# Scores mixed into the first inverse product of a tile, the last slot's rows turned on TensorE, zero rows held back during a weight load, and one activation issued earlier

## What is computed

```
x = x + attn(layernorm(x))        # x is 1 x 2048 x 512
  q, k, v = silu(conv4(x @ Wq)), silu(conv4(x @ Wk)), silu(conv4(x @ Wv))   # 8 heads of 64
  q, k = l2norm(q) / 8, l2norm(k); beta = sigmoid(x @ Wb)
  per token: u = beta * (v - k S);  S = S + k^T u;  o = q S
  o = o * rsqrt(mean(o*o)) * norm_w;  attn = o @ Wo
x = x + ffn(layernorm(x))
  routed: softmax gate, 2 of 4 groups, top 4 of 16 experts, (silu(x Wg) * (x Wu)) @ Wd, width 352
  shared: the same form with width 704, for every token
```

## Time and profile before

| | us |
|---|---|
| median of 3 runs | 1335.73 (1335.23 to 1336.11) |
| the profiled execution, its own time | 1335.12 |
| its span, first to last instruction | 1333.4 |
| PE busy | 1280.4 (96% of the span) |
| DVE / ACT / POOL busy | 870.3 / 373.6 / 336.8 |
| PE's granted clock, mean over the span | 0.983 of full speed |

### The profile page before, as it was taken

The page is one execution under the profiler, slowest core; times in us unless marked ns, Lnnn a source line. Parts: engine busy times, 40 slices in busy tenths (PEclk is TensorE's granted clock), DMA queues, the critical chain, the costliest instruction groups (busy, mean ns, idle before and its releaser), DMA issues.

```text
span 1333.4 us, 27815 instructions
## 1 busy us (share of the span) xinstructions
PE 1280.4 (96%) x8722; PEld 797.3 (60%) x8723; DVE 870.3 (65%) x2426; ACT 373.6 (28%) x816; POOL 336.8 (25%) x396
## 2 busy tenths in 40 slices
PE   8978999998998999999999999999999999999996
PEld 7857777776776555444444555555555555555553
DVE  4896698669659325645111577777777777777774
ACT  4745555555453323120000011111111111111111
POOL 1211224322233122214653012122121222212121
PEclk9989999999997999999999999999999999999997
DMA  5525852743467494265456556666665656564420
GB/s 160 97 42 103 122 118 70 154 117 74 106 135 172 121 236 106 99 212 209 177 204 232 131 128 132 137 132 139 135 138 130 135 132 134 128 139 71 71 51 1
DMA packets 208515, 171.08 MB, mean 128 GB/s; under 512 B 71472, under 2 KB 160560, under 8 KB 208432
## 3 DMA queue, kind: packets, MB, share of 16 engines
q1 hardware_dynamic: 135056, 114.16, 33.4%
q0 software_dynamic: 16496, 34.23, 13.1%
q10 hardware_dynamic: 56880, 21.54, 7.8%
HBM read 91.06 MB, written 82.73 MB: 130 GB/s over the span
## 4 chain that ended last, share of the span: by engine, by line
PE 54%; DVE 2%; issue 0%; POOLq 0%; DVEq 0%; ACT 0%
PE pD L2202 15%; PE pG L2182 14%; PE pU L2191 14%; PE pG L2146 3%; PE pU L2146 3%; PE pD L2165 3%; DVE ups L2092 1%; PE pU L2140 1%; PE pD L2160 0%; POOLq L1917 0%; DVE w L1804 0%; DVE w L1805 0%; DVE route_keep L1803 0%; DVE qf L1816 0%; DVE q L1823 0%
## 5 line engine op out<-in xcount | busy, mean ns | idle before, releaser
L2092 DVE STREAM_TRANSPOSE ups<-a 32x96 f32<-32x96 f32 (+1 forms) x1264 | 330.4, 261 | 42.7
L1989 POOL DMA_INDIRECT out<-y,ix x79 | 123.0, 1557 | 481.3 <-ACT y L2045 322.7
L2202 PE MATMUL pD<-w,ups 128*128 (+1 forms) x474 | 219.3, 599 | 3.6 <-DVE ups L2092 3.6
L2182 PE MATMUL pG<-w,xsT 128*128 x632 | 199.9, 458 | 0.0
L2191 PE MATMUL pU<-w,xsT 128*128 x632 | 199.9, 459 | 0.0
L2182 PEld LDWEIGHTS pG<-w,xsT 128*128 128x128 f32 x632 | 119.5, 189 | 88.4 <-issue 37.6
L2191 PEld LDWEIGHTS pU<-w,xsT 128*128 128x128 f32 x632 | 120.1, 190 | 66.9
L954 PE MATMUL pProj<-front_region 128*128 128x256 f32 x624 | 154.5, 390 | 2.0 <-ACT front_region L697 1.6
L2202 PEld LDWEIGHTS pD<-w,ups 128*128 128x128 f32 (+1 forms) x474 | 90.8, 192 | 98.0 <-issue 81.7
L1331 DVE SCALAR_TENSOR_TENSOR front_region<-front_region,cw 128x256 f32<-128x256 f32 x288 | 133.4, 504 | 12.3 <-ACT front_region L733 8.9
L2045 ACT ACTIVATE y<-pD,wq 128x512 f32<-128x512 f32 x79 | 54.3, 687 | 255.2 <-PE pD L2202 245.5
(11 more groups left out here) (240 smaller groups left out, 1575.9 us busy)
## 6 DMA issues: line engine op xcount, KB each, us to landing
w<-in_up_T SPq DMA_DIRECT2D x16, 1408.0 KB, 6.8
slot_rows<-zeros SPq DMA_DIRECT2D x79, 266.0 KB
xs<-slot_rows ACTq DMA_DIRECT2D x316, 64.0 KB
w<-in_down_T SPq DMA_DIRECT2D x16, 512.0 KB, 8.8
front_region<-in_L_attn_hidden_states SPq DMA_DIRECT2D x16, 256.0 KB, 3.5
x2r<-in_L_attn_hidden_states SPq DMA_DIRECT2D x16, 256.0 KB, 4.8
partial_sums<-x2r SPq DMA_DIRECT2D x16, 256.0 KB, 3.7
x_normed<-x2n SPq DMA_DIRECT2D x16, 256.0 KB, 2.2
```

The costliest lines, as they stand in the source:

```text
L1989: pool.indirect_dma_start(out=flat, out_offset=bass.IndirectOffsetOnAxis(ap=ix[1 - par][:, 0:1], axis=0), in_=y[1 - par][:, :], in_offset= ...
L2092: dve.transpose(aT[par][B * to:B * to + B, 0:n, rows], a[rows, 0:len(IC) * P].rearrange("p (c n) -> p c n", c=len(IC))[:, 0:n, B * to:B * ...
L2182: mm = pe.matmul(pG[0][:, 0:I], xsT[par][:, k, :], w[:, bass.ds(slot, 1), 2 * I * k:2 * I * k + I], start=(k == 0), stop=(k == DC - 1))
L2202: mm = pe.matmul(pYq[:, :], aT[1 - par][0:m, c, :], down[0:m, :, UPW + D * c:UPW + D * (c + 1)], start=(c == 0), stop=(c == 2))
```

## The change

Four edits, independent of each other.

1. `scores(u+1)` no longer stands alone ahead of the projection. For u from 0 to 14 its 16 matmuls are placed between the 8 of `hop_u(u, 0)`, in a new function `hop_u_and_scores`. DVE's `mask_scores(u+1)` moves from the end of slot 1 to the start of slot 2.
2. For the last slot PE turns the rows of `a` itself with three transposes against an identity (`turn_last`), placed in the down product of the slot before; ACT and DVE copy the results; the last down product has a bank of its own (`pYlast`). POOL builds the identity after its routing constants.
3. `zero_rows` is not called in step 10 from slot 2 on, nor in step 11 in slots 0 and 1. Six pieces move to the end of the list: step 15 slot 1 and step 16 slots 0 to 4.
4. `shared_silu` stands ahead of the copies of its slot on ACT.

```diff
-                    if u >= 0 and not (u % 4 == 3 and s >= 2) and not (u % 4 == 1 and s >= 4) and not (u % 4 == 2 and s < 1):
+                    if u >= 0 and not (u % 4 == 3 and s >= 2) and not (u % 4 == 1 and s >= 4) and not (u % 4 == 2 and s < 1) \
+                            and not (u == 10 and s >= 2) and not (u == 11 and s < 2):
                         zero_rows()
...
+                    for n in range(EARLY_UNITS):
+                        if fill_slot(u, s) == event_slot(gate_end(n)):
+                            shared_silu(n)
                     if tile_ok(u) and s == 0 and u < FUSED:
                         x_copy(u)
...
+            def hop_u_and_scores(t):
+                if t < FUSED:
+                    pe.wait_ge(s_TT, t + 1)
+                else:
+                    pe.wait_ge(s_X, 2 * t + 2)
+                pe.wait_ge(s_R, 2 * t + 1)
+                scores_wait(t + 1)
+                r = cols(0, C)
+                for n in range(HH):
+                    for f, between in ((0, ((1, 1), (0, 0), (1, 0))), (1, ((0, 1),))):
+                        g = HH * f + n
+                        u_mm = pe.matmul(pC[r, f, cols(n)], TT[t % TT_RING][r, cols(g)], Rs[r, cols(g)], start=True, stop=True)
+                        if (n, f) == (HH - 1, 1):
+                            u_mm.then_inc(s_Up, 1)
+                        for sf, sc in between:
+                            s_mm = score(t + 1, n, sf, sc)
+                s_mm.then_inc(s_Pp, 1)
...
-                    if s == 1 and tile_ok(u + 1):
-                        scores(u + 1)
+                    if s == 1 and u == -1:
+                        scores(0)
...
-                    if tile_ok(u) and s in (1, 4):
+                    if s == 1 and tile_ok(u) and tile_ok(u + 1):
+                        hop_u_and_scores(u)
+                    elif tile_ok(u) and s in (1, 4):
                         hop_u(u, s // 3)
...
+                    if s == 2 and tile_ok(u) and tile_ok(u + 1):
+                        mask_scores(u + 1)
...
-                    if s == 1 and tile_ok(u + 1):
-                        mask_scores(u + 1)
+                    if s == 1 and u == -1:
+                        mask_scores(0)
...
+    pA, pYlast = [pG[1], pU[1], pD[3]], pD[1]
...
+                if isinstance(q, int) and q == NQ - 1:
+                    act.wait_ge(s_yp, NQ - 2)
+                    for c in (0, 2):
+                        act.wait_ge(s_lap, c + 1)
+                        act.activation(aT[par][0:IC[c], c, :], pA[c][0:IC[c], 0:P], ACT.Copy).then_inc(s_laT, 1)
...
-                    turn_gated(q, par)
+                    if isinstance(q, int) and q == NQ - 1:
+                        dve.wait_ge(s_yp, NQ - 2)
+                        dve.wait_ge(s_lap, 2)
+                        dve.tensor_copy(aT[par][:, 1, :], pA[1][:, 0:P]).then_inc(s_laT, 1)
+                    else:
+                        turn_gated(q, par)
...
+            def turn_last():
+
+                pe.wait_ge(s_eye, 2)
+                pe.wait_ge(s_a, NQ)
+                for c in range(3):
+                    pe.transpose(pA[c][0:IC[c], 0:P], a[:, P * c:P * c + IC[c]], eye[:, :]).then_inc(s_lap, 1)
...
                     for c in range(3):
                         m = IC[c]
-                        mm = pe.matmul(pYq[:, :], aT[1 - par][0:m, c, :], down[0:m, :, UPW + D * c:UPW + D * (c + 1)],
+                        if isinstance(q, int) and q == NQ - 1 and c == 2:
+                            turn_last()
+                        mm = pe.matmul((pYlast if end(q) else pYq)[:, :], aT[1 - par][0:m, c, :], down[0:m, :, UPW + D * c:UPW + D * (c + 1)],
                                        start=(c == 0), stop=(c == 2))
```

More of the change, by code:

```diff
@@ L905, in _ @@
                         w_copy(u + 1)
-                    for n in range(EARLY_UNITS):
-                        if fill_slot(u, s) == event_slot(gate_end(n)):
-                            shared_silu(n)
                     if (u, s) == ROUTE_AT:
@@ L1008, in gram, with scores_wait, score @@
                 mm.then_inc(s_G, 1)
+            def scores_wait(t):
+                least(pe, s_N, capped(t + 5 if t % 2 and not late_gram(t - 2) else t + 4))
+            def score(t, n, f, c):
+                p = t // 2
+                return pe.matmul(pG[cols(c, C), f, cols(n)], kq[p % KQ_RING][half(f), n, tok(t, c)],
+                                 kq[p % KQ_RING][half(f), DC + n, tok(t, c)], start=True, stop=True)
             def scores(t):
-                p = t // 2
-                least(pe, s_N, capped(t + 5 if t % 2 and not late_gram(t - 2) else t + 4))
+                scores_wait(t)
                 for n in range(HH):
@@ L1015, in scores @@
                         for f in range(2):
-                            mm = pe.matmul(pG[cols(c, C), f, cols(n)], kq[p % KQ_RING][half(f), n, tok(t, c)],
-                                           kq[p % KQ_RING][half(f), DC + n, tok(t, c)], start=True, stop=True)
+                            mm = score(t, n, f, c)
                 mm.then_inc(s_Pp, 1)
@@ L1849, in experts @@
     g, a = sb("g", [P, I]), sb("a", [P, len(IC) * P])
+    eye = sb("eye", [P, P])
     y = [sb(f"y{i}", [P, D]) for i in range(2)]
@@ L1867, in experts @@
     s_add, s_ex, s_base = sem("rows_added"), sem("meta_taken"), sem("base_stored")
+    s_eye, s_lap, s_laT = sem("identity2"), sem("last_gated_psum"), sem("last_gatedT_ready")
     s_xT, s_gp, s_g, s_up, s_a, s_aT, s_yp, s_y = (sem(n) for n in (
@@ L1965, in _ @@
             route_pool(pool)
+            pool.memset(eye[:, :], 0.0).then_inc(s_eye, 1)
+            pool.wait_ge(s_eye, 1)
+            pool.affine_select(out=eye[:, :], in_=eye[:, :], compare_op=ALU.not_equal, fill=1.0,
+                               base=0, pattern=[[-1, P]], channel_multiplier=1).then_inc(s_eye, 1)
             for n in BY_POOL:
@@ L2044, in body @@
                         act.wait_ge(s_add, (q - 2) * 16)
-                    act.activation(y[1 - par][:, :], pYq[:, :], ACT.Copy, scale=wq[1 - par][:, 0:1]).then_inc(s_y, 1)
+                    act.activation(y[1 - par][:, :], (pYlast if end(q) else pYq)[:, :], ACT.Copy, scale=wq[1 - par][:, 0:1]).then_inc(s_y, 1)
             route_act(act)
@@ L2195, in body @@
                 if not first(q):
-                    pe.wait_ge(s_aT, BLOCKS * BLOCKS * q)
-                    wait_pos(pe, s_y, q - 1)
+                    if end(q):
+                        pe.wait_ge(s_laT, 3)
+                    else:
+                        pe.wait_ge(s_aT, BLOCKS * BLOCKS * q)
+                        wait_pos(pe, s_y, q - 1)
                     if isinstance(q, int) and q == 1:
```

## The result

| | before | after |
|---|---|---|
| median, us | 1334.78 (19 runs) | 1327.67 (19 runs) |
| ratio, 95% interval | | 0.9947 (0.9939 to 0.9955) |
| profiled execution, us | 1335.12 | 1325.61 |
| granted clock in it | 0.983 | 0.988 |

A forecast was written before the change was run, and what follows sets the result against it. PE, the engine with least idle time, was taken to bound the kernel, except where DVE's inverse does. Savings of 0.5 (mix and mask), 0.9 (step 11) and 2.3 us (tail) sum to 3.7: forecast 1331.9 us, range 1328.6 to 1335.1.

The forecast's parts named there:

- The mix on PE: Attention: hop_u and scores interleaved take 1.55 us, saving 0.14 us per tile; eight steps keep it, 1.1 us.
- halves: Rival for the mixed products: matmuls of one row half don't overlap, 2.10 us per mix, slower at 1338.7; chance 0.04.
- Step 2: Attention: DVE's mask waits for the mixed scores, idling 0.5 us; 0.6 us lost, passing through to PE's wait at merge_w.
- Edit 1: 1.1 - 0.6: Attention: 1.1 us from eight mixed products less 0.6 us lost to the late mask in step 2; 0.5 us saved.
- keep nothing: Attention steps 3, 7 and 11 end in a wait for DVE or the inverse, so they keep none of the mix's saving.
- Edits 3 and 4: Step 11: load and silu waits, 2.6 us together, go; the inverse allows only 0.9 us, a wait over 1 us appears at L1026.
- The tail: Last slot: turning on PE puts the last two adds 5.62 us apart instead of 8.36, slot 77's 0.45 later; 2.3 us saved.
- The clock rival: Before tile 12 PE waits 1.7 us, the clock falls, costing up to 6 us: 1337.9; chance 0.06.

The follow-up runs named there:

- e7_mask: The kernel before with only DVE's mask moved to the start of slot 2, PE's order unchanged; 1331.74 us, ratio 0.9975 against before.
- e10_maskback: The changed kernel with DVE's mask back at the end of slot 1, products still mixed; 1335.12 us, ratio 1.0004 against before.
- r_after: The changed kernel measured again, unaltered, beside a version with the scores apart on the same chip; 1328.54 us, ratio 0.9945 against before.
- e34_load: The kernel before with only the held-back zero pieces and the earlier silu; 1336.61 us, ratio 1.0005 against before.
- e6_fill7: The kernel before with 8 repeated matmuls ahead of PE's wait for the residual in step 7; 1334.36 us, ratio 0.9998 against before.
- e15_warm3: The kernel before with three useless matmuls on PE while DVE turns the last slot's rows; 1333.65 us, ratio 0.9986 against before.
- e9_fill: The changed kernel with extra matmuls ahead of waits in step 3 (6) and step 10 (2); 1330.07 us, ratio 0.9968 against before.
- e12_all: The changed kernel, scores apart and mask early in steps 2, 10, 11, extra matmuls in steps 3, 10, transposes behind slot 77's product; 1332.96 us, 0.9977 against before.
- e17_part: The changed kernel, scores apart and mask at slot 1's end in steps 2, 10, 11, three extra matmuls in steps 3, 7; 1326.69 us, 0.9935 against before.

## Why the prediction was off

- **The mix on PE**: 1.55 us predicted, 1.54 measured, so *halves* (2.10) fell. The Trainium skill (TensorE: Matmul & The Clock Gate, section Part 3: Packing small matmuls) says that a weight load overlaps with running matmuls only when the row group differs; 1.54 us is less than the 2.10 of *halves*, so as that rule was used there it does not hold for these alternating columns. The saving of 0.14 us is right for even steps; in odd ones it is 0.35, because the neighbours of the moved projection changed as well: 0.6 us more over steps 1, 5 and 9. Another 0.3 us came in step 6, where PE's wait for x2r fell from 1.04 to 0.72 us. It takes both halves of the edit: the wait is 1.03 us in e7_mask and 1.00 in e10_maskback.
- **Step 2**: DVE idles 0.58 us before the mask (0.5 predicted). The wait of tile 4 at `merge_w` was 1.47 us in r_after, and absent in the first profile, where the clock fell instead. That the loss goes through was right, and its size was more: in the mean of the four kernels with edit 1 step 3 takes 32.1 us, 0.9 more than in the six with the old order, where 0.6 was priced.
- **The step that failed: "Edit 1: 1.1 - 0.6".** Edit 1 gave 4.1 us (2.9 to 5.5), not 0.5. The sum priced the mask's move by the one step in which it is late, and at nothing elsewhere, and it let steps 3 and 7 "keep nothing". In both the new place lies beside osb. DVE reaches the residual 0.67 us sooner in each than with the mask back (11.46 against 12.13 us after the gate, after and e10_maskback), and the clock seems to fall less often behind the shorter wait. Step 7 gained 1.5 us by this; in step 3 the mix's losses outweighed it. The cue stood in the trace before: prod_b at 1.80 us where an equal one takes 0.95, and the 3.17 us wait of step 7 with half the clock behind it, neither of which I read. The rest of the miss is in the other term: 1.1 us for eight mixes at 0.14. Steps 4, 5, 6 and 8 alone gave 1.5, and the mixes of odd steps, those of the excluded steps 3 and 7 too, save 0.35 each.
- **Edits 3 and 4**: the waits at L1138 and L1151 went and one of 1.04 us came at L1026, as said ("over 1 us"), but PE also waits 1.99 us (1.04 in r_after) for the scaled TT: the mix asks for it before the scores, which used to fill 0.6 us of that wait. The profile of e34_load has 0.8 us of the 0.9 (50.28 us from the gate of step 10 to that of step 12, 51.08 before), and after 0.3. But other executions with the old order there take 49.97 (e6_fill7) to 51.81 us (e15_warm3), and the median of e34_load is not told from no change. So whether the 0.9 is right isn't shown.
- **The tail: a mis-sized term.** The mechanism held to the step (landing, not y, released the add; slot 77's add 0.33 us later, 0.45 predicted). The landing was priced at 5.62 us from start to start by the mean of ten waits, all of full slots; the last slots are empty, and it was 3.63. The 8.36 us on the other side was a long case, which hid a part of this error: 3.4 us in the usual one, 4.4 against the profile that the sum used, not 2.3.
- **The clock rival** priced a fall behind the wait before tile 12. It did not come in the first profile and did in r_after (a wait of 1.67 us, then step 11 at 30.55 us instead of 28.67), inside a kernel that is faster all the same.

```profile
448.62 0.69 PE L1033 MATMUL pT<-TT,NP 32*32 32x32 f32 x32 [1.67 <-DMA TT<-inverse_turned]
```

## What to carry to other kernels

When an operation moves on one engine, ask in every step what now runs beside it, on the other engines too. If GpSimd holds DVE's operations on two SBUF inputs off, an operation that reads PSUM is the one to put there: here it cost nothing. A price taken from a mean of waits is good only for the same work: the last slots of a padded schedule are often empty, and here the same DMA is 2 us cheaper there. A profile of one execution shows one throw of the clock; before pricing a stretch with half the clock, see in other executions how often it comes.

## What had not been expected of the hardware

- An indirect add whose indices are all out of bounds still takes 2.7 us from issue to landing, a full one of 128 rows 4.6 to 5.0 in most slots.
- GpSimd's osb (128x512, 1.04 us alone) makes DVE's 128x768 product take 1.80 instead of 0.95 us, or else the convolution behind it 3.49 instead of 2.70; a product with one input in PSUM (0.68) is as long beside it as alone.
- Waits of 2.5 us in step 7 left the clock at 1.00 in eight of twelve executions, and one of 2.00 us in step 3 did not; work that changes nothing, put ahead of a wait, kept it at 1.00 behind that wait each time (e6_fill7, e9_fill, e12_all, e17_part).
